# Cross-attention scores on TensorE: from six stacked bf16 parts on 96 rows to three fp32r parts on 48 rows, with two heads in the two row halves of the array

## The chip, the cores and the metric

One core of a Trainium2 chip runs the program. The metric is the device time of one execution in microseconds; lower is better. The engines are named as in the profile: PE (TensorE, with PEld for its weight loads), DVE (VectorE), ACT (ScalarE), POOL (GpSimd), SP (SyncE, which here only issues DMAs).

## The reference, cut to what matters

Four batches of 512 rows of 256 features go through an attention layer and then a mixture of experts with a shared expert. The attention keys and values come from a context (1601 rows, of which the causal mask leaves the first 512 in use).

```
Q = (layernorm(x) @ Wq.T + bq), K = (ctx @ Wk.T + bk), V = (ctx @ Wv.T + bv)   # 16 heads of 16
scores = einsum('bhqd,bhkd->bhqk', Q, K) / sqrt(16);  scores = where(causal, scores, -inf)
x = x + softmax(scores) @ V @ Wo.T + bo
logits = layernorm(x) @ gate_w.T;  two of eight experts per row, softmax weights
x = x + shared(layernorm(x)) + sum over the two experts of weight * (silu(g) * u) @ w_down[e].T
```

All tensors are fp32. The scores are wanted near fp32 precision, which is why Q and K are split into parts of lower precision whose products are added up.

## The kernel before

The program is written engine by engine, with semaphores set by hand; the order of the work on each engine is the order of the code. It has a prologue (loads, layer norm, transposes, first projections), the attention of the four batches (batches 0 to 2 in a hardware loop `Fori`, batch 3 as the final one), the router, and the expert stage.

**Groups and slots.** The 16 heads are four groups of four. A batch has four slots; in slot g PE makes the scores of group g, the row maxima of group g + 1, and P times V of group g - 1. The order inside is written out by hand in `SLOT` (L312): "R" is a row-maximum job, "S" a scores job, "PV" a quarter of P times V, "MAX" the maxima.

**The parts.** A projection of a half (128 features, two groups) lands in PSUM; DVE adds the bias (`values`, L1211) into `val`. ACT rounds it to bf16 (`part1`, L983), POOL subtracts (`remainders`, L502), ACT rounds the rest (`part2`, L993), POOL subtracts again (`part3`, L507), so Q and K are three bf16 parts each. In the prologue DVE makes the subtractions (L1218, L1223) between its row maxima. SP copies the parts by DMA from SBUF to SBUF into `qstack` and `kstack` (`stack`, L380): six products of parts, 16 features each, are stacked on 96 rows, so that one matmul over 96 rows gives the whole score. That is 12 DMAs for one group. A projection is made in slots g = 1 and g = 3 (a "split slot" in what follows); its stacks for the two groups go out there and in the slot behind. SP works in order: in `batch` (L403) stacks and `max_rows` alternate.

**Row maxima.** `rowmax_scores` (L601) makes the scores of a query tile k with queries on the partitions, `w = (k + 1) * 128` keys wide, and adds the mask to the diagonal block by a second matmul of two bf16 constants (L611). Its jobs fill half of set A of PSUM, two banks: k = 3 and k = 2 two heads a job, k = 1 and k = 0 four heads: six jobs. DVE reduces each (`rowmax`, L1252), and `max_parts` (L1264) splits the negated maxima into three bf16 parts in four steps. `maxima` (L614) transposes them by four matmuls on the identity into a bank of set B; ACT copies that (`max_rows`, L1009); SP writes it by DMA into rows 96 to 98 of `qstack` (L392), against rows of ones in `kstack` (filled at L483). S0 of the next slot waits for that DMA (`max_in`, L709).

**Scores and P V.** `scoresT` (L623) makes the scores with keys on the partitions, over 99 rows, so the maximum is already subtracted; ACT takes the exponential of each job into `pT` (`exps`, L1018). There are 11 S jobs: 4 of one head 512 wide, 4 of one head 384 wide, 2 of two heads 256 wide, 1 of four heads 128 wide. B jobs (S and MAX) rotate over three banks, and job n waits until job n - 3 is read (`b_free`). POOL zeroes the diagonal blocks (L524), and `probs_v` (L633) multiplies with V in fp32, each of the four heads on its own 32 columns of the array. ACT copies that out at the place MAX_AT = 9 of its own order (`p_v`, then `max_rows`).

**Output stage** of a batch: transposes of the output (L790), division by the sums on DVE (L1318, L1320), V of the next batch (L651), transposes back in `A_TILES` groups of three, three and two (L799), and the output projection (L815). In the final batch ACT also rounds the down weights (`down_hi`, L1013).

## Time and profile before

| what | us |
|---|---|
| median of 3 runs | 526.19 (525.32 to 528.68) |
| the profiled execution | 527.34 |
| its span, first to last instruction | 525.6 |
| PE matmul busy | 461.9 (88%) |
| DVE busy | 315.5 (60%) |
| ACT busy | 209.9 (40%) |
| POOL busy | 192.6 (37%) |
| mean granted PE clock, share of full speed | 0.962 |

The shown length of a matmul includes the time in which its last columns run through the array, so matmuls overlap; what one costs in a stream is the distance from its start to the next one's start. A weight load (PEld) is shown beside the matmuls. "x8" on a timeline row means eight instructions merged, from the first start to the last end. A time in brackets is how long the engine was idle before, and who released it. An fp32 matmul shows as two records.

### The profile page before, as it was taken

What the parts mean: (1) busy time and instruction counts of PE and PEld (TensorE: products, weight loads), DVE (VectorE), ACT (ScalarE), POOL (GpSimd) and SP (SyncE); (2) the same over time, 40 slices, a digit from 0 to 9 for tenths busy, and PEclk for the clock granted to TensorE, in tenths of its full rate; (3) what the DMA queues carried; (4) which work ended last, traced back from release to release, by engine and by line L of the source; (5) the groups of instructions that cost most, each with busy time, mean ns of one, the idle gap of its engine ahead of it and who ended that gap; (6) DMA issues with size and microseconds to landing.
All of it is one profiled execution on the core that took longest, in us unless ns stands there. A gap on an engine that the chain in (4) does not pass through costs nothing.

```text
span 525.6 us, 9951 instructions
## 1 busy us (share of the span) xinstructions
PE 461.9 (88%) x2998; PEld 314.7 (60%) x2999; DVE 315.5 (60%) x655; ACT 209.9 (40%) x421; POOL 192.6 (37%) x196
## 2 busy tenths in 40 slices
PE   3636989799898998988869999999999999999993
PEld 1315434365443744355326355669999999999942
DVE  6756666546656375756655489585545555555537
ACT  1213555542656255641785343333223232323210
POOL 8003543311334143510230100313766676766430
PEclk9956999989999999999998999999999999999997
DMA  8521331131112412130059760102444434444379
GB/s 255 211 73 44 97 105 68 60 129 60 66 65 71 141 39 83 50 127 24 3 188 343 295 228 1 42 10 42 67 74 63 76 64 70 70 72 69 42 178 332
DMA packets 45575, 53.84 MB, mean 102 GB/s; under 512 B 7761, under 2 KB 41873, under 8 KB 44913
## 3 DMA queue, kind: packets, MB, share of 16 engines
q1 hardware_dynamic: 35360, 40.63, 22.7%
q0 software_dynamic: 7488, 10.31, 12.2%
q10 hardware_dynamic: 2704, 2.62, 1.4%
q8 instruction: 13, 0.21, 0.2%
q14 instruction: 10, 0.07, 0.0%
HBM read 27.09 MB, written 13.67 MB: 78 GB/s over the span
## 4 chain that ended last, share of the span: by engine, by line
PE 63%; DVE 8%; ACT 8%; DMA 7%; issue 6%; SPq 4%; POOL 2%; DVEq 0%; ACTq 0%; POOLq 0%
PE set_a L902 5%; PE set_a L904 5%; PE set_a L903 5%; PE set_a L609 5%; PE set_a L834 5%; PE set_a L660 4%; ACT attention L1028 4%; PE set_b L639 4%; SPq L389 4%; PE set_b L629 4%; DMA attention<-attention 3%; PE set_b L844 3%; PE set_b L921 3%; PE set_a L815 3%; PE set_b L923 2%
## 5 line engine op out<-in xcount | busy, mean ns | idle before, releaser
L1262 DVE TENSOR_REDUCE attention<-set_a 128x2 f32<-128x1024 f32 (+2 forms) x96 | 96.2, 1042 | 37.2 <-PE set_a L611 35.7
L1028 ACT ACTIVATE attention<-set_b 128x512 f32<-128x512 f32 (+1 forms) x176 | 87.9, 566 | 62.7 <-PE set_b L629 62.3
L524 POOL TENSOR_SCALAR_AFFINE_SELECT attention<-attention 128x512 f32<-128x512 f32 x64 | 41.7, 663 | 113.6 <-ACT attention L1028 113.5
L629 PE MATMUL set_b<-attention 99*128 99x512 bf16 (+3 forms) x256 | 60.9, 313 | 20.2 <-ACT attention L1028 9.8
L609 PE MATMUL set_a<-attention 96*128 96x512 bf16 (+3 forms) x256 | 64.4, 317 | 16.2 <-DVE attention L1262 8.4
L575 POOL DMA_INDIRECT sum_rows<-moe,token_of x39 | 61.8, 1585 | 44.0 <-issue 29.9
L567 POOL DMA_INDIRECT e_x<-normed_rows,token_of x39 | 39.4, 1011 | 65.6 <-DVE token_of L1468 39.2
L1133 ACT ACTIVATE moe<-set_a 128x384 f32<-128x384 f32 x39 | 19.1, 490 | 105.3 <-PE set_a L904 97.3
L609 PEld LDWEIGHTS set_a<-attention 96*128 96x128 bf16 x256 | 26.1, 102 | 57.0 <-DVE attention L1262 21.7
L1493 DVE TENSOR_TENSOR moe<-set_a,moe 128x384 f32<-128x384 f32 x39 | 21.8, 558 | 62.7 <-issue 39.5
L902 PE MATMUL set_a<-wup_hi,e_xT_hi 128*128 x156 | 53.2, 341 | 0.0
L904 PE MATMUL set_a<-wup_hi,e_xT_lo 128*128 x156 | 52.8, 339 | 0.0
L903 PE MATMUL set_a<-wup_lo,e_xT_hi 128*128 x156 | 52.8, 338 | 0.0
L611 PE MATMUL set_a<-maskb,identb 128*128 128x128 bf16 x256 | 51.6, 229 | 0.0
L639 PE MATMUL set_b<-attention 128*32 128x128 f32 (+3 forms) x512 | 45.9, 460 | 0.7 <-ACT attention L974 0.7
L629 PEld LDWEIGHTS set_b<-attention 99*128 99x128 bf16 x256 | 19.7, 100 | 44.6 <-ACT attention L1028 24.2
L660 PE MATMUL set_a<-attention 128*128 (+1 forms) x64 | 30.8, 625 | 9.1 <-DMA attention<-in_ctxT 7.9
L921 PE MATMUL set_b<-w_down_hi,e_hT_hi 128*128 x117 | 36.5, 312 | 1.1 <-DVE moe L1505 0.9
L974 ACT ACTIVATE attention<-set_b 12x512 bf16<-12x512 f32 (+4 forms) x48 | 25.8, 598 | 26.9 <-PE set_b L803 13.2
L974 ACT ACTIVATE attention<-attention 128x512 bf16<-128x512 f32 x32 | 19.5, 645 | 39.8 <-DVE attention L1214 31.1
L923 PE MATMUL set_b<-w_down_hi,e_hT_lo 128*128 x117 | 32.9, 282 | 0.0
L922 PE MATMUL set_b<-w_down_lo,e_hT_hi 128*128 x117 | 32.9, 281 | 0.0
...
## 6 DMA issues: line engine op xcount, KB each, us to landing
...
```

Source lines behind the costliest of these rows:

```text
L575: g.indirect_dma_start(acc[i], bass.IndirectOffsetOnAxis(token_of[:, t:t + 1], 0), e_y[:, t % 2, :], None, compute_op=ALU.add).then_inc(ad ...
L609: mm(dst, qstack[0:ROWS, g // 2, h, k * P:w], kstack[0:ROWS, g // 2, h, 0:w], start=True, stop=False)
L611: last = mm(dst[:, k * P:w], identb[:], maskb[:], start=False, stop=True)
L629: last = mm(bank(par)[:, i * w:(i + 1) * w], kstack[0:ROWS + 3, g // 2, h, k * P:(k + 1) * P], qstack[0:ROWS + 3, g // 2, h, k * P:S], sta ...
L639: last = mm(pv_bank[32 * h:32 * h + 32, k * P:S], vaug[:, k, HG * g + h, :], pT[k][:, h, :], start=k == 0, stop=k == QT - 1, tile_position ...
L660: last = mm(pair(A, par)[:, a, :], w[:, c, half * P:(half + 1) * P], src[:, c, bass.ds(b * S, S)], start=c == 0, stop=c == C - 1)
L902: mm(dst, e_xT_hi[:, a, c, :], wup_hi[:, c, cols], start=c == 0, stop=False)
L903: mm(dst, e_xT_hi[:, a, c, :], wup_lo[:, c, cols], start=False, stop=False)
L904: last = mm(dst, e_xT_lo[:, a, c, :], wup_hi[:, c, cols], start=False, stop=c == C - 1)
L921: mm(dst, e_hT_hi[:, a, m, :], wdn_hi[:, m, cols], start=m == 0, stop=False)
L1028: nc.scalar.activation(pT[k][:, h:h + heads, :], bank(par)[:, 0:heads * (S - k * P)], ACT.Exp).then_inc(b_free, 1)
L1262: v.tensor_reduce(dst, src, AX.X, ALU.max, negate=True).then_inc(a_free, 1)
```

## The change

1. Q and K are split into two parts in fp32r, high and low: one ACT copy (`hi_parts_of`) and one subtraction (`low_parts`). The stack has three products (high-high, low-high, high-low) of 16 features: 48 rows. `part2`, `part3` and their waits are gone. The packing of the weights (`by_group`) changes so that a group's heads lie in pairs.
2. Two heads share the array: heads of the upper pair lie on rows 0 to 47 of `qstack` and `kstack`, those of the lower on rows 64 to 111. `rowmax_scores` issues the matmuls of two heads one behind the other, each on its row half and into its own PSUM bank, then their two mask matmuls over all rows. A stack is again 12 DMAs of a group, of 32 source rows of fp32.
3. The maxima are split into two fp32r parts; their rows are 48 and 49 of each half, over 50 rows in `scoresT`; two DMAs instead of one carry them.
4. There are 12 S jobs, each on one row half; the one of four heads at k = 3 becomes two of two. `SLOT` is reordered: S0, S1, S2 follow R2 without a row-maximum job between them.
5. `kstack` is filled whole with ones before the stacks; SP waits for that once (`fills`). `identr`, a copy of the identity in fp32r, is made by ACT in the prologue; PE waits for it once. `A_TILES` is two groups of four. `probs_v` takes its heads in the new order, and S0 waits for 2 x 16 more of `max_in` per slot. The stacks lie at fixed fp32r tensors in the same region.

The diff, cut to its core, blank lines left out and most lines moved left:

```diff
@@ -70,10 +70,11 @@
...
     SCALE = float(DK) ** -0.5
-    Q_PART = (0, 0, 1, 1, 0, 2)
-    K_PART = (0, 1, 0, 1, 2, 0)
+    Q_PART = (0, 1, 0)
+    K_PART = (0, 0, 1)
     ROWS = DK * len(Q_PART)
-    assert S == 512 and D == 256 and H == 2 * HH and ROWS == 96
+    HIGH = P // 2
+    assert S == 512 and D == 256 and H == 2 * HH and ROWS == 48 and HG == 4
@@ -163,17 +175,10 @@
...
 pT = [pT_all[:, pT_at[k]:pT_at[k + 1]].rearrange("p (h q) -> p h q", h=HG) for k in range(QT)]
-qstack = part(2 * HH * S // 2).bitcast(BF16).rearrange("p (a h n) -> p a h n", a=2, h=HH)
-kstack = part(2 * HH * S // 2).bitcast(BF16).rearrange("p (a h n) -> p a h n", a=2, h=HH)
+part(STACKS)
 val = part(2 * S).rearrange("p (a n) -> p a n", a=2)
-rem = part(2 * S).rearrange("p (a n) -> p a n", a=2)
-parts = part(2 * 3 * S // 2).bitcast(BF16).rearrange("p (a i n) -> p a i n", a=2, i=3)
-mneg = part(QT * HG).rearrange("p (k h) -> p k h", k=QT)
-mrem = part(QT * HG).rearrange("p (k h) -> p k h", k=QT)
-mparts = part(QT * 3 * HG // 2).bitcast(BF16).rearrange("p (k i h) -> p k i h", k=QT, i=3)
-mrows = part(S // 2).bitcast(BF16)
+mneg = part(QT * HG).rearrange("p (k a r) -> p k a r", k=QT, a=2)
 vaug = part(QT * H * 32).rearrange("p (k h w) -> p k h w", k=QT, h=H)
@@ -282,36 +287,23 @@
 stored = sem("stored")
-def heads_in_pair(k):
-    return max(2, min(HG, 1024 // ((k + 1) * P)) & ~1)
-def heads_in_bank(k):
-    return 1 if k < 2 else min(HG, 512 // (S - k * P))
-R_JOBS = [(k, h, heads_in_pair(k)) for k in range(QT - 1, -1, -1) for h in range(0, HG, heads_in_pair(k))]
+R_JOBS = [(3, (0,)), (3, (1,)), (2, (0,)), (2, (1,)), (1, (0, 1)), (0, (0, 1))]
 A_GRP = len(R_JOBS)
...
 A_ALL = A_PRO + B * A_PER - 2 * A_GRP - 3
-S_JOBS = [(k, h, heads_in_bank(k)) for k in range(QT) for h in range(0, HG, heads_in_bank(k))]
+S_JOBS = [(k, a, pr, 1 if k < 2 else 2) for k in range(QT)
+          for pr in (range(2) if k < 2 else range(1)) for a in range(2)]
 S_N = len(S_JOBS)
 B_SLOT = S_N + 1
-SLOT = [("R", 0), ("PV", 0), ("R", 1), ("PV", 1), ("R", 2),
-        ("S", 0), ("R", 3), ("S", 1), ("R", 4), ("S", 2), ("S", 3), ("R", 5), ("S", 4), ("S", 5),
-        ("S", 6), ("S", 7), ("PV", 2), ("PV", 3), ("S", 8), ("MAX", 0), ("S", 9), ("S", 10)]
+SLOT = [("R", 0), ("PV", 0), ("R", 1), ("PV", 1), ("R", 2), ("S", 0), ("S", 1), ("S", 2), ("R", 3),
+        ("S", 3), ("R", 4), ("S", 4), ("R", 5), ("S", 5), ("S", 6), ("S", 7), ("PV", 2), ("PV", 3),
+        ("S", 8), ("MAX", 0), ("S", 9), ("S", 10), ("S", 11)]
 LOGITS_IN = [A[:, 0, :], A[:, 1, :], pv_bank, A[:, 0, :]]
@@ -319,7 +311,7 @@
...
 assert [n for kind, n in SLOT if kind == "S"] == list(range(S_N))
-A_TILES = [range(i, min(i + 3, C * QT)) for i in range(0, C * QT, 3)]
+A_TILES = [range(i, i + 4) for i in range(0, C * QT, 4)]
 NA = len(A_TILES)
@@ -379,21 +371,24 @@
     def stack(g, u):
-        half, mine = g // 2, slice(g % 2 * 64, g % 2 * 64 + 64)
-        heads = slice(g % 2 * HG, g % 2 * HG + HG)
-        for part, made in enumerate((part1_ready, part2_ready, parts_ready)):
+        for part, (made, src) in enumerate(((hi_ready, qk_hi), (lo_ready, qk_lo))):
             for a, (dst, order) in enumerate(((qstack, Q_PART), (kstack, K_PART))):
...
                 for j, part_of in enumerate(order):
-                    if part_of == part:
-                        sp.dma_start(dst[DK * j:DK * (j + 1), half, heads, :],
-                                     parts[mine, a, part, :]).then_inc(rows_in[g], DMA)
+                    for high in range(2):
+                        if part_of == part:
+                            to, frm = HIGH * high + DK * j, HIGH * (g % 2) + 32 * high
+                            sp.dma_start(dst[to:to + DK, 2 * g:2 * g + 2, :].bitcast(F32),
+                                         src[frm:frm + 32, a, :].bitcast(F32)).then_inc(rows_in[g], DMA)
     def max_rows(g, n):
         sp.wait_ge(b_free, n + 1)
-        h = g % 2 * HG
-        sp.dma_start(qstack[ROWS:ROWS + 3, g // 2, h:h + HG, :], mrows[0:3 * HG, :]).then_inc(max_in, DMA)
+        for high in range(2):
+            to = HIGH * high + ROWS
+            sp.dma_start(qstack[to:to + 2, 2 * g:2 * g + 2, :].bitcast(F32),
+                         mrows[HG * high:HG * (high + 1), :].bitcast(F32)).then_inc(max_in, DMA)
+    sp.wait_ge(fills, 1)
     stack(0, 0)
@@ -480,7 +475,7 @@
     pool.wait_ge(consts, 4)
-    g.memset(kstack[ROWS:P], 1.0).then_inc(fills, 1)
+    g.memset(kstack[:].bitcast(F32), 1.0).then_inc(fills, 1)
     pool.wait_ge(fills, 1)
@@ -499,25 +494,16 @@
...
         pool.sem_inc(pool_turns)
-    def remainders(u):
+    def low_parts(u):
         for a in range(2):
-            pool_turn(part1_ready, 2 * u + a + 1)
-            g.tensor_tensor(rem[:, a, :], val[:, a, :], parts[:, a, 0, :], ALU.subtract).then_inc(rem_ready, 1)
-    def part3(u):
-        for a in range(2):
-            pool_turn(part2_ready, 2 * u + a + 1)
-            g.tensor_tensor(parts[:, a, 2, :], rem[:, a, :], parts[:, a, 1, :],
-                            ALU.subtract).then_inc(parts_ready, 1)
+            pool_turn(hi_ready, 2 * u + a + 1)
+            g.tensor_tensor(qk_lo[:, a, :], val[:, a, :], qk_hi[:, a, :], ALU.subtract).then_inc(lo_ready, 1)
     def mask_group(n, last=False, split=None):
         if split is not None:
-            remainders(split)
+            low_parts(split)
         for k in range(QT):
-            if k == 2 and split is not None:
-                part3(split)
             jobs = sum(job[0] <= k for job in S_JOBS)
@@ -600,15 +586,16 @@
     def rowmax_scores(g, j, n, par):
         pe.wait_ge(a_free, n - 1)
-        k, h0, heads = R_JOBS[j]
+        k, prs = R_JOBS[j]
         w = (k + 1) * P
-        in_bank = heads // 2 if k else HG
-        for i in range(heads):
-            h = g % 2 * HG + h0 + i
-            dst = pair(A, par)[:, i // in_bank, i % in_bank * w:(i % in_bank + 1) * w]
-            mm(dst, qstack[0:ROWS, g // 2, h, k * P:w], kstack[0:ROWS, g // 2, h, 0:w],
-               start=True, stop=False)
-            last = mm(dst[:, k * P:w], identb[:], maskb[:], start=False, stop=True)
+        for i, pr in enumerate(prs):
+            for high in range(2):
+                rows = slice(HIGH * high, HIGH * high + ROWS)
+                mm(pair(A, par)[:, high, i * w:(i + 1) * w], qstack[rows, 2 * g + pr, k * P:w],
+                   kstack[rows, 2 * g + pr, 0:w], start=True, stop=False, tile_position=(HIGH * high, 0))
+            for high in range(2):
+                last = mm(pair(A, par)[:, high, i * w + k * P:(i + 1) * w], identb[:], maskb[:],
+                          start=False, stop=True)
         last.then_inc(a_full, 1)
     def maxima(n, par, g_count, first=False):
@@ -616,18 +603,19 @@
...
         for k in range(QT):
-            last = mm(bank(par)[0:3 * HG, k * P:(k + 1) * P],
-                      mparts[:, k].rearrange("p i h -> p (i h)"), identb[:], start=True, stop=True)
+            last = mm(bank(par)[0:2 * HG, k * P:(k + 1) * P],
+                      mparts[:, k].rearrange("p a i r -> p (a i r)"), identr[:], start=True, stop=True)
         last.then_inc(b_full, 1)
     def scoresT(g, j, n, par):
         pe.wait_ge(b_free, n - 2)
-        k, h0, heads = S_JOBS[j]
+        k, high, pr, heads = S_JOBS[j]
         w = S - k * P
+        rows = slice(HIGH * high, HIGH * high + ROWS + 2)
         for i in range(heads):
-            h = g % 2 * HG + h0 + i
-            last = mm(bank(par)[:, i * w:(i + 1) * w], kstack[0:ROWS + 3, g // 2, h, k * P:(k + 1) * P],
-                      qstack[0:ROWS + 3, g // 2, h, k * P:S], start=True, stop=True)
+            last = mm(bank(par)[:, i * w:(i + 1) * w], kstack[rows, 2 * g + pr + i, k * P:(k + 1) * P],
+                      qstack[rows, 2 * g + pr + i, k * P:S], start=True, stop=True,
+                      tile_position=(HIGH * high, 0))
         last.then_inc(b_full, 1)
     def probs_v(g, count, k):
@@ -637,7 +625,7 @@
...
             last = mm(pv_bank[32 * h:32 * h + 32, k * P:S], vaug[:, k, HG * g + h, :],
-                      pT[k][:, h, :], start=k == 0, stop=k == QT - 1, tile_position=(0, 32 * h))
+                      pT[k][:, h % 2 * 2 + h // 2, :], start=k == 0, stop=k == QT - 1, tile_position=(0, 32 * h))
         if k == QT - 1:
@@ -988,37 +977,33 @@
...
             act.wait_ge(*((val_ready, u + 1), (a_free, n + 1))[a])
-            copy(parts[:, a, 0, :], val[:, a, :]).then_inc(part1_ready, 1)
-    def part2(u):
-        for a in range(2):
-            act.wait_ge(rem_ready, 2 * u + a + 1)
-            copy(parts[:, a, 1, :], rem[:, a, :]).then_inc(part2_ready, 1)
+            copy(qk_hi[:, a, :], val[:, a, :]).then_inc(hi_ready, 1)
     def ln_copy(b):
...
     ln_copy(0)
-    part1(0, 0)
-    part2(0)
+    hi_parts_of(0, 0)
+    act.wait_ge(consts, 1)
+    copy(identr[:], ident[:]).then_inc(identr_ready, 1)
     deviations(1, QT, T)
-    part1(1, 1, ((0, 1), 1))
-    part2(1)
+    hi_parts_of(1, 1, ((0, 1), 1))
     def max_rows(n, par):
         act.wait_ge(b_full, n + 1)
-        copy(mrows[0:3 * HG, :], bank(par)[0:3 * HG, :]).then_inc(b_free, 1)
+        copy(mrows[0:2 * HG, :], bank(par)[0:2 * HG, :]).then_inc(b_free, 1)
     def down_hi(i):
...
         copy(down_piece(wdn_hi, i), down_piece(wdn, i)).then_inc(dn_hi, 1)
-    def exps(n, par, pv=None, rows=True, split=None, down={}):
-        for j, (k, h, heads) in enumerate(S_JOBS):
+    def exps(n, par, pv=None, rows=True, down={}):
+        for j, (k, high, pr, heads) in enumerate(S_JOBS):
+            h = 2 * high + pr
             if pv and j == MAX_AT:
@@ -1215,24 +1197,18 @@
...
             last.then_inc(a_free if a else val_ready, 1)
-    def remainders(u):
+    def low_parts(u):
         for a in range(2):
-            dve.wait_ge(part1_ready, 2 * u + a + 1)
-            v.tensor_tensor(rem[:, a, :], val[:, a, :], parts[:, a, 0, :], ALU.subtract).then_inc(rem_ready, 1)
-    def part3(u):
-        for a in range(2):
-            dve.wait_ge(part2_ready, 2 * u + a + 1)
-            last = v.tensor_tensor(parts[:, a, 2, :], rem[:, a, :], parts[:, a, 1, :], ALU.subtract)
-            last.then_inc(parts_ready, 1)
+            dve.wait_ge(hi_ready, 2 * u + a + 1)
+            v.tensor_tensor(qk_lo[:, a, :], val[:, a, :], qk_hi[:, a, :], ALU.subtract).then_inc(lo_ready, 1)
     statistics(0)
...
     values(0, 0, 0)
-    remainders(0)
-    part3(0)
+    low_parts(0)
+    dve.wait_ge(lo_ready, 2)
     values(1, 1, 1)
     def add_v(n, par):
@@ -1250,37 +1226,26 @@
...
     def rowmax(j, n, par):
-        k, h, heads = R_JOBS[j]
+        k, prs = R_JOBS[j]
         dve.wait_ge(a_full, n + 1)
-        if k:
-            src = pair(A, par)[:, :, 0:heads // 2 * (k + 1) * P].rearrange("p a (h n) -> p a h n",
-                                                                         h=heads // 2)
-            dst = mneg[:, k, h:h + heads].rearrange("p (a h) -> p a h", a=2)
-        else:
-            src = pair(A, par)[:, 0, :].rearrange("p (h n) -> p h n", h=HG)
-            dst = mneg[:, k, :]
-        v.tensor_reduce(dst, src, AX.X, ALU.max, negate=True).then_inc(a_free, 1)
+        src = pair(A, par)[:, :, 0:len(prs) * (k + 1) * P].rearrange("p a (r n) -> p a r n", r=len(prs))
+        v.tensor_reduce(mneg[:, k, :, prs[0]:prs[0] + len(prs)], src, AX.X, ALU.max,
+                        negate=True).then_inc(a_free, 1)
     def max_parts(n, g_count):
         dve.wait_ge(a_free, n)
-        s0 = (g_count - 1) * 3
-        v.tensor_copy(mparts[:, :, 0, :], mneg).then_inc(mpart_step, 1)
-        dve.wait_ge(mpart_step, s0 + 1)
-        v.tensor_tensor(mrem, mneg, mparts[:, :, 0, :], ALU.subtract).then_inc(mpart_step, 1)
-        dve.wait_ge(mpart_step, s0 + 2)
-        v.tensor_copy(mparts[:, :, 1, :], mrem).then_inc(mpart_step, 1)
-        dve.wait_ge(mpart_step, s0 + 3)
-        v.tensor_tensor(mparts[:, :, 2, :], mrem, mparts[:, :, 1, :], ALU.subtract).then_inc(mparts_ready, 1)
+        hi = mparts[:, :, :, 0, :]
+        v.tensor_copy(hi, mneg).then_inc(mpart_step, 1)
+        dve.wait_ge(mpart_step, g_count)
+        v.tensor_tensor(mparts[:, :, :, 1, :], mneg, hi, ALU.subtract).then_inc(mparts_ready, 1)
     for g in range(2):
...
             if g == 0 and j == 1:
-                remainders(1)
-            if g == 0 and j == 3:
-                part3(1)
+                low_parts(1)
         max_parts(3 + (g + 1) * A_GRP, g + 1)
```

## Rows read from the trace of the kernel before

**Rows 1.** The page: busy by engine; the chain that ended last

```profile
PE 461.9 (88%) x2998; PEld 314.7 (60%) x2999; DVE 315.5 (60%) x655; ACT 209.9 (40%) x421; POOL 192.6 (37%) x196
PE 63%; DVE 8%; ACT 8%; DMA 7%; issue 6%; SPq 4%; POOL 2%; DVEq 0%; ACTq 0%; POOLq 0%
```

**Rows 2.** Windows: length, busy us (PE, PEld, DVE, ACT, POOL), clock, DMA share, GB/s

```profile
97.60:112.40 14.80, 12.17 (x88) 5.70 (x85) 6.98 (x10) 6.68 (x15) 3.77 (x6) 0.77 0.24 81
161.10:172.20 11.10, 9.53 (x89) 4.44 (x86) 6.93 (x10) 6.61 (x15) 3.74 (x6) 1.00 0.27 95
```

**Rows 3.** Timeline of PE, batch 1: start, length in us, what was run

```profile
126.19 0.38 PE L609 MATMUL set_a<-attention 96*128 96x512 bf16 x1
126.41 0.22 PE L611 MATMUL set_a<-maskb,identb 128*128 128x128 bf16 x1
126.47 0.38 PE L609 MATMUL set_a<-attention 96*128 96x512 bf16 x1
126.69 0.22 PE L611 MATMUL set_a<-maskb,identb 128*128 128x128 bf16 x1
126.84 1.07 PE L639 MATMUL set_b<-attention 128*32 128x512 f32 x8
135.00 0.39 PE L619 MATMUL set_b<-identb,attention 128*12 128x128 bf16 x4
136.51 0.38 PE L609 MATMUL set_a<-attention 96*128 96x512 bf16 x1
```

**Rows 4.** Waits: us in total, times, longest

```profile
PE set_b L629 <- DMA attention<-attention: 9.3, 7, 2.5
PEld set_b L629 <- ACT attention L1028: 24.2, 50, 1.2
```

**Rows 5.** Timeline of all engines, same slot and the next start

```profile
127.72 5.98 DVE L1262 TENSOR_REDUCE attention<-set_a 128x2 f32<-128x1024 f32 x6
134.54 1.19 ACT L974 ACTIVATE attention<-attention 128x512 bf16<-128x512 f32 x2
135.48 2.27 POOL L510 TENSOR_TENSOR attention<-attention 128x512 bf16<-128x512 f32 x2
139.11 0.79 SPq L395 DMA_DIRECT2D attention<-attention  x1
141.43 0.39 PE L629 MATMUL set_b<-attention 99*128 99x512 bf16 x1 [1.22 <-DMA attention<-attention]
```

**Rows 6.** Timeline of all engines, end of the slot from 136.51 on

```profile
146.32 0.39 PE L619 MATMUL set_b<-identb,attention 128*12 128x128 bf16 x4
146.92 1.05 ACT L974 ACTIVATE attention<-set_b 128x512 f32<-128x512 f32 x2
147.31 1.08 PE L660 MATMUL set_a<-attention 128*128 x2
147.99 0.75 SPq L395 DMA_DIRECT2D attention<-attention  x1
```

**Rows 7.** Timeline of PE: 8-row transposes, then a full-array matmul

```profile
300.78 0.41 PE L746 MATMUL set_a<-ident,moe 8*128 8x8 f32 x4 [0.68 <-ACT moe L974]
301.12 1.13 PE L834 MATMUL set_a<-moe,w_sg 128*128 128x512 f32 x2
```

**Rows 8.** Timeline of PE in the expert stage, fp32r matmuls of 256 columns

```profile
420.81 0.38 PE L921 MATMUL set_b<-w_down_hi,e_hT_hi 128*128 x1
421.02 0.28 PE L922 MATMUL set_b<-w_down_lo,e_hT_hi 128*128 x1
421.14 0.28 PE L923 MATMUL set_b<-w_down_hi,e_hT_lo 128*128 x1
```

**Rows 9.** Timeline of POOL and DVE in the prologue

```profile
3.11 6.92 POOL L483 MEMSET attention<- 32x8192 bf16 x1
...
39.94 1.28 DVE L1226 TENSOR_TENSOR attention<-attention 128x512 bf16<-128x512 f32 x2
```

**Rows 10.** Timeline of PE, start of a slot in the final batch

```profile
254.89 0.38 PE L609 MATMUL set_a<-attention 96*128 96x512 bf16 x1
```

33 lines of the change are left out of this document (21 added, 12 removed).

## The prediction

> **What bounds the kernel now.** I read the page first, then the windows by stage, then TensorE's timeline inside one attention slot, then the list of waits. The page gives TensorE 88% of the span and the chain that ended last puts 63% on it [rows 1]. The change touches attention alone, which ends near 276 us, so everything behind it stays. In attention one batch is four slots of 10.3 to 11.1 us (161.1 to 172.2 is one, 126.19 to 136.51 another [rows 2, 3]) and an output stage.
>
> Inside a slot TensorE goes in order through row-maximum jobs (R), scores jobs (S), probabilities times V (PV) and the maxima. Its prices, from starts in [rows 3]: a bf16 matmul of 512 columns takes 0.22 us (126.19 to 126.41), a mask matmul of 128 columns 0.06 (126.41 to 126.47). From the last mask (126.69, done streaming at 126.75) to PV (126.84) lie 0.09 us in which nothing streams: the array goes from all columns to four groups of 32. PV's eight records are two passes of four heads that start together, about 0.43 each at 512 columns: tiles of the array do run side by side here. So R0, PV0, R1, PV1, R2 up to S0 are 0.56 + 0.85 + 0.56 + 0.64 + 0.45, and four switches of 0.09: 3.4 us. From R0 to the end of the last maxima matmul (I call that M; a 128-column matmul is shown with 0.17 us behind its streaming, so M is 135.22) are 9.0 us.
>
> Two slots of each looped batch hold a wait on top. PE's wait for the DMA of the maxima rows is 9.3 us over 7 times; its loads wait for ACT's exps for 24.2 us, 1.5 a slot over 16 slots [rows 4]. Its cause is in [rows 5]: ACT makes the second parts at 134.54, GpSimd the third at 135.48 (2.27 us), only then can SyncE issue the last stack DMAs, and the maxima row DMA queued behind them goes at 139.11; S0 starts at 141.43 after a 1.22 us wait. In batch 0 the wait was the longest (2.5 us), and the granted clock of that stretch is 0.77 against 1.00 [rows 2]: 14.8 us where the same slot of batch 1 took 11.1. That slot lost 3.7 us more, about 1.3 of it wait and 2.4 the 1.2 GHz level that the clock fell to after the idle time.
>
> **Removed from the path.** No second pair of copies on ACT (1.3 us of a split slot's 2.6), no third part on GpSimd, two of four DVE steps of the maxima. The stack DMAs stay 12 per unit and 64 KB each, so SyncE still issues 12 x 0.64 us, but the last four wait for GpSimd's single subtraction, which can end about 3 us after ACT's first copies start; the third parts end at 137.75, more than 7 us later. The maxima DMA (two now, +0.64 us of issue) then starts when ACT's copy is done. In [rows 6] that copy pair (0.45 + 0.6) ends at 147.97, 1.4 us after M (146.54); two issues and a 2.2 us landing give S0 at M + 4.4, while PE needs until about M + 5.2. So the waits go: 1.2 us in each of six slots, and in batch 0 the 3.7.
>
> **Added on TensorE.** A pair of fp32r matmuls on the two row halves, then two full-array masks. Does a change of row grouping cost a gap like the column one? The only case is in [rows 7]: transposes on 8 rows, the last starting at 300.78 + 0.41 - 0.20 = 300.99 with 8 columns to stream, then a full-array matmul that waits for nothing, at 301.12: 0.13 us, of which the 8 columns explain at most some 0.03. I take 0.09 per switch; bounds 0 and 0.13. fp32r costs 0.12 us per 256 columns [rows 8], so 0.24, 0.18, 0.12, 0.06 for 512 to 128; and where the weight load could not go ahead (420.81) the next matmul came after 0.21, not 0.12: 0.09 to 0.10 us for an exposed load, bounds 0 and 0.10. Masks with their bf16 load: 0.13 a pair.
>
> By this, two heads cost 0.24/0.18/0.12/0.06 + 0.09 + 0.13, and 0.09 + 0.10 to come back to the row mode: 0.65, 0.59, 0.53, 0.47 us, against 0.56, 0.45, 0.34, 0.23 now. Over eight pairs of a slot: 4.5 against 3.2, less two PV switches that were paid already (0.2): +1.1 us. Loads exposed at S8 and S9: +0.2. Scores stream 5,120 columns at 0.47 against 0.43 ns, less one pair that overlaps (S0, S1; the others are apart in the order or gated by ACT): no change. Work +1.3 us a slot.
>
> The Trainium skill, TensorEngine Tiling (Array Packing), Key Properties, states that changing the tiling mode, not just the tile, drains TensorE. The 0.09 us of [rows 3, 7] agree with it; by a reading without drains the sum would be the first rival's. The same skill, TensorE: Matmul & The Clock Gate, Weight-path perf modes, keeps the fast weight load from fp32 operands; the 0.10 us of [rows 8] agrees.
>
> Last, an added wait. There are 12 S jobs rather than 11, over three banks, so S11 reuses the bank of the maxima and must wait for ACT's copy, M + 1.4 by [rows 6]. Behind it in PE's queue are the projection and the next R0. Now they start at M + 0.8 (147.31); then at M + 1.6: +0.8. In split slots (g = 1, 3) the second copies already delay ACT; the next R0 comes at M + 1.3 (136.51), so +0.3.
>
> **Sum.** R0 to S0 is then 3.55 us. From S0 to M: S0 to S2 0.48, R3 and back 0.59, S3 0.24, R4 1.06, S4 0.18, R5 0.94, S5 to S7 0.54, PV2 and PV3 with both switches 0.88 and a load 0.10, S8, switch and maxima 0.57: 5.6. R0 to M is 9.15 of work, against 9.0 of which some 0.9 was waiting for ACT, which the new work takes up; an unsplit slot (136.51 to 146.54, less its 1.22 wait) took 8.8. So a split slot is +0.15 + 0.3, +0.45. Slot g = 2: +0.35 + 0.8 - 1.2, 0. Slot g = 0, where the output stage starts after ACT's PV copy, 1.1 behind M now and 1.6 then: +0.35 + 0.5 - 1.15, -0.3. Output stage, two transposed groups instead of three: -0.1. A batch: +0.5. Batches 1 and 2: +1.0; batch 0: +0.5 - 3.7 = -3.2. Prologue: the two part-3 subtractions (1.28) and half of the small steps go [rows 9], but the R4 and R5 behind run at 1.2 GHz with the added switches: -0.5. Its larger-looking fill of kstack is 4,096 four-byte elements a partition where 8,192 took 6.92 us from 3.11, long before the first stack at 19 us: 0. Final batch, no split, ACT also makes w_down_hi: R0 started at 254.89 right after S10 [rows 10]; S11 waits for the copy that ends near 255.5, so +0.85 for two slots and +0.2 in the third: +1.9. Total +1.0 - 3.2 - 0.5 + 1.9 = -0.8 us. The profiled execution took 527.34 us, 1.7 of it outside its span of 525.6, so by it the sum gives 526.5; it was 1.15 above the median of the runs, 526.19, so against that I forecast 525.4.
>
> **Rivals.** (A) No drain for row groups and loads prefetched: 14 added switches x 0.09 and 10 loads x 0.10, 2.3 us of PE work less a slot. DVE's six row maxima (6.0 us [rows 5]) and S11 then bound it: unsplit slots gain 1.6, six times, the others 0.5, nine times: 525.4 - 14 = 511. For: no row shows 64-row tiles. Against: [rows 7]. (B) The halves do not overlap: R streams 1.2 us more and S0/S1 0.24, in 16 slots: +22, 547. Against: PV's four tiles start together. (C) Slower through the clock: array streaming in a slot falls from about 7.7 us to 6.3 of 10.7, more gaps; if the granted clock falls as it did at 103 us, at 2.4 us each, in two slots of each of the three looped batches, +14: 539. It decides once the clock is below 1.00 in slots where nothing waits. For: the dip of [rows 2]. Against: waits of 1.2 us made none. (D) The ACT and GpSimd chain, not PE, sets the split slots: 1.3 us of copy, 0.4 of DVE and the waits of S6, S7 and S10 go, the new work fits in: -1.3 in six slots: 517.5. For: PE's loads wait 1.5 us a slot for ACT. Against: the work is at 8.1 us of 9.0 there before 1.1 is added ahead of M.
>
> **Numbers.** Forecast 0.45, A 0.15, B 0.10, C 0.15, D 0.15. The forecast's own range is 519 to 532. Low 512 takes in D and half of A, high 543 takes in C and leaves B out. A measurement tells about 1% here, 5.3 us. Faster: A, D and a little of the forecast, 0.33; slower: B, C and a little, 0.29; within 1%: 0.38.
>
> **What would show it.** Granted clock 1.00 through 97 to 112 us and that slot near 11; no PE wait for the maxima DMA; last R matmul to first mask 0.09 us more than streaming; a pair's two starts within some 0.01 us; PE waiting for ACT's copy ahead of the last S job; split slots near 10.8, slot g = 2 near 10.8. If masks follow without a gap, A holds; if the second head starts a stream later, B; if the clock row is below 1.00 in looped batches, C. Slots under 10 us or over 12 make the prediction wrong.

## The result and the profile after

| | median us | runs | ratio to the kernel before, 95% interval |
|---|---|---|---|
| before | 526.68 | 525.32 to 528.68 | |
| after | 563.51 | 555.61 to 567.16 | 1.0646 [1.053, 1.0763] |

The change makes the kernel 6.5% slower; the forecast was 525.4 and its range ended at 543. The four executions of the kernel after took 567.16, 563.90, 563.12 and 555.61 us at a mean granted clock of 0.876, 0.884, 0.885 and 0.905: the lower the clock, the longer the time. The profiled one is the slowest of them, 3.6 us above the median, and its losses are read with that in mind. The granted clock is the share of full speed that TensorE was given, between 1.00 (2.4 GHz) and 0.50 (1.2 GHz); a value between them is the mean of a stretch that had both.

The page of the kernel after: busy times, the row of the granted clock (40 slices of the span, in tenths), the chain that ended last, and the groups of the row maxima, their masks and the scores.

```profile
PE 518.2 (92%) x2998; PEld 347.0 (61%) x2999; DVE 304.9 (54%) x619; ACT 204.5 (36%) x418; POOL 177.5 (31%) x184
...
PEclk9957699559658899986958799999999999999998
...
PE 78%; ACT 6%; DMA 4%; DVE 4%; issue 3%; SPq 3%; DVEq 0%; ACTq 0%; POOLq 0%
...
L594 PE MATMUL set_a<-kstack,qstack 48*128 48x512 f32 (+3 forms) x256 | 70.8, 448 | 15.0 <-DVE attention L1232 7.8
L616 PE MATMUL set_b<-qstack,kstack 50*128 50x256 f32 (+3 forms) x256 | 76.8, 456 | 8.2 <-ACT mrows L963 5.6
```

PE has as many instructions as before (2998), is 56 us longer busy, and its share of the chain went from 63% to 78% [rows 1]. No other engine took anything over: DVE, ACT and POOL are all less busy. So it is PE that runs longer, and the clock row says how. In the kernel before it reads

```profile
PEclk9956999989999999999998999999999999999997
```

with one dip inside attention. After, 14 of the first 23 slices are below 9. Two stretches of the same length in both, batch 0 and batch 1 (columns: start and end, length, busy us of PE, PEld, DVE, ACT and POOL, granted clock, DMA share, GB/s). The kernel before:

```profile
66.00:118.00 52.00, 45.91 (x353) 23.80 (x352) 28.89 (x45) 28.30 (x58) 17.61 (x23) 0.93 0.26 89
118.00:172.00 54.00, 49.54 (x377) 24.39 (x375) 33.76 (x50) 29.13 (x61) 17.75 (x22) 1.00 0.19 66
```

The kernel after, with three shorter stretches:

```profile
66.00:118.00 52.00, 50.55 (x319) 23.77 (x317) 28.21 (x34) 24.39 (x51) 13.20 (x17) 0.83 0.28 70
118.00:172.00 54.00, 53.17 (x267) 30.83 (x265) 20.94 (x31) 19.34 (x41) 9.53 (x13) 0.66 0.21 59
...
98.90:145.00 46.10, 45.52 (x238) 26.74 (x239) 20.52 (x30) 15.94 (x34) 7.61 (x10) 0.70 0.25 71
...
101.00:112.00 11.00, 10.74 (x59) 4.58 (x60) 3.28 (x6) 3.83 (x9) 1.91 (x3) 0.50 0.26 63
...
239.00:250.00 11.00, 10.44 (x87) 5.34 (x86) 7.76 (x10) 6.96 (x14) 3.78 (x4) 1.00 0.30 72
```

The last two are the same kind of work, 11 us each: at clock 1.00 PE gets 87 matmuls done in them, at 0.50 (the 1.2 GHz level) 59. And in the slow one PE is not idle: it is busy for 10.74 of 11.00 us. This is the main reading of the case: the clock is at its lower level although PE works without a pause.

Where the 39.8 us of span went (565.4 less 525.6). Slots are counted here from R0 to the next R0, where in the kernels with row halves R0 starts with the second matmul of its pair; slot g = 2 thus includes the projection of the slot behind it. 4.8 us were lost before the first row maxima of slot g = 1 of batch 0 (50 to 62.7 us is at clock 0.62, where it was at 1.00 before), 29.1 in the twelve slots from there to the final batch's slot g = 1, 2.5 in that slot and 3.4 behind it. Where a slot ran at clock 1.00 throughout it is near the forecast: a split slot 11.00 us against 10.31 before, slot g = 2 with the projection 14.66 against 14.28. Where it did not, the same slots took up to 12.92 (clock 0.76) and 22.79 (0.54). At the end of a split slot the first matmul of the pair starts 0.18 us ahead of the second, beside the last scores job on the other row half (249.80 and 249.98 below). Counted to that first start the two slots are 10.82 and 14.85 us; their sum is the same to 0.01 us.

Inside a slot at full clock. The timeline of PE in the kernel after, slot g = 3 of batch 2:

```profile
238.97 0.50 PE L594 MATMUL set_a<-kstack,qstack 48*128 48x512 f32 x2
239.41 0.28 PE L597 MATMUL set_a<-maskb,identb 128*128 128x128 bf16 x2
239.62 1.06 PE L627 MATMUL set_b<-attention 128*32 128x512 f32 x8
240.62 0.51 PE L594 MATMUL set_a<-kstack,qstack 48*128 48x512 f32 x2
...
242.64 0.73 PE L616 MATMUL set_b<-qstack,kstack 50*128 50x512 f32 x3
...
248.01 0.41 PE L606 MATMUL set_b<-identr,mparts 128*8 128x128 f32 x4
248.34 0.86 PE L616 MATMUL set_b<-qstack,kstack 50*128 50x256 f32 x4
249.71 0.32 PE L616 MATMUL set_b<-qstack,kstack 50*128 50x128 f32 x1 [0.51 <-ACT mrows L963]
249.80 0.49 PE L594 MATMUL set_a<-kstack,qstack 48*128 48x512 f32 x1
...
249.98 0.44 PE L594 MATMUL set_a<-kstack,qstack 48*128 48x512 f32 x1
```

Two heads together take 0.50 us; shown one by one at the start of the next slot they take 0.49 and 0.44: the row halves do run side by side. From the pair's start to the first mask are 0.44 us, of which streaming is 0.24. S0 comes 3.67 us behind R0, the maxima are done at 248.01 + 0.41 - 0.17 = 248.25, and PE then stands idle for 0.51 us before the last scores job. The list of waits of the kernel after agrees (us in total, times, longest):

```profile
PE set_b L616 <- ACT mrows L963: 5.6, 14, 0.5
PE set_b L616 <- ACT attention L1013: 1.9, 5, 0.6
```

There is no wait for the DMA of the maxima rows in it, which was 9.3 us before [rows 4]; the new wait for ACT's copy is 5.6 us over 14 slots.

### The profile page after: what moved, and what is told of

Read it like the earlier page. It is cut to its first block, busy times and chain, and to the rows that moved or that the text cites. A ratio compares the mean times of both kernels' runs of the same rounds, so it can differ in the third digit from the quotient of the medians.

```text
span 565.4 us, 9891 instructions
## 1 busy us (share of the span) xinstructions
PE 518.2 (92%) x2998; PEld 347.0 (61%) x2999; DVE 304.9 (54%) x619; ACT 204.5 (36%) x418; POOL 177.5 (31%) x184
## 3 DMA queue, kind: packets, MB, share of 16 engines
q0 software_dynamic: 7488, 10.31, 11.5%
## 4 chain that ended last, share of the span: by engine, by line
PE 78%; ACT 6%; DMA 4%; DVE 4%; issue 3%; SPq 3%; DVEq 0%; ACTq 0%; POOLq 0%
PE set_b L627 9%; PE set_b L616 9%; PE set_a L594 7%; PE set_a L648 6%; PE set_a L597 5%; PE set_a L891 5%; PE set_a L893 5%; PE set_a L892 5%; PE set_a L823 4%; PE set_b L833 3%; PE set_b L910 3%; PE set_a L804 3%; SPq L381 2%; PE set_b L912 2%; ACT attention L1013 2%
## 5 line engine op out<-in xcount | busy, mean ns | idle before, releaser
L1232 DVE TENSOR_REDUCE attention<-set_a 128x2 f32<-128x1024 f32 (+2 forms) x96 | 98.4, 1044 | 62.1 <-PE set_a L597 61.0
L594 PE MATMUL set_a<-kstack,qstack 48*128 48x512 f32 (+3 forms) x256 | 70.8, 448 | 15.0 <-DVE attention L1232 7.8
L616 PE MATMUL set_b<-qstack,kstack 50*128 50x256 f32 (+3 forms) x256 | 76.8, 456 | 8.2 <-ACT mrows L963 5.6
L594 PEld LDWEIGHTS set_a<-kstack,qstack 48*128 48x128 f32 x256 | 34.8, 217 | 54.8 <-DVE attention L1232 27.8
L616 PEld LDWEIGHTS set_b<-qstack,kstack 50*128 50x128 f32 x256 | 41.7, 233 | 30.6 <-ACT attention L1013 10.2
L627 PE MATMUL set_b<-attention 128*32 128x128 f32 (+3 forms) x512 | 58.2, 566 | 0.0
L648 PE MATMUL set_a<-attention 128*128 (+1 forms) x64 | 36.4, 721 | 8.4 <-DMA attention<-in_ctxT 7.3
L597 PE MATMUL set_a<-maskb,identb 128*128 128x128 bf16 x256 | 41.2, 250 | 0.0
L597 PEld LDWEIGHTS set_a<-maskb,identb 128*128 128x128 bf16 x256 | 15.3, 102 | 29.8 <-issue 25.4
L1196 DVE TENSOR_SCALAR attention<-set_a,attention 128x512 f32<-128x512 f32 x16 | 11.3, 747 | 38.9 <-PE set_a L648 38.8
```

The lines of the kernel that those rows point to most:

```text
L594: mm(pair(A, par)[:, high, i * w:(i + 1) * w], qstack[rows, 2 * g + pr, k * P:w], kstack[rows, 2 * g + pr, 0:w], start=True, stop=False, t ...
L597: last = mm(pair(A, par)[:, high, i * w + k * P:(i + 1) * w], identb[:], maskb[:], start=False, stop=True)
L616: last = mm(bank(par)[:, i * w:(i + 1) * w], kstack[rows, 2 * g + pr + i, k * P:(k + 1) * P], qstack[rows, 2 * g + pr + i, k * P:S], start ...
L627: last = mm(pv_bank[32 * h:32 * h + 32, k * P:S], vaug[:, k, HG * g + h, :], pT[k][:, h % 2 * 2 + h // 2, :], start=k == 0, stop=k == QT - ...
L648: last = mm(pair(A, par)[:, a, :], w[:, c, half * P:(half + 1) * P], src[:, c, bass.ds(b * S, S)], start=c == 0, stop=c == C - 1)
L1232: v.tensor_reduce(mneg[:, k, :, prs[0]:prs[0] + len(prs)], src, AX.X, ALU.max, negate=True).then_inc(a_free, 1)
```

## Experiments: what lowers the clock

The theory that I began with (C1): the clock falls because of the short gaps that 14 changes of array mode and 10 exposed weight loads put into each slot. Its rivals: the number of array rows that work (C2: 48 and 50 of 128 in the new matmuls, 96 and 99 before), the wait of the last scores job, and fp32r itself. Where a kernel below runs the matmuls of a pair over the rows of both halves, it leaves out the right scores: both heads get the sum of the two. Such a kernel is there to be timed only.

**Both matmuls over the rows of both halves.** The query stack is filled with zeros and the unused rows 48 to 63 of the key stack too.

```diff
-                        rows = slice(HIGH * high, HIGH * high + ROWS)
+                        rows = slice(0, HIGH + ROWS)
                         mm(pair(A, par)[:, high, i * w:(i + 1) * w], qstack[rows, 2 * g + pr, k * P:w],
-                           kstack[rows, 2 * g + pr, 0:w], start=True, stop=False, tile_position=(HIGH * high, 0))
+                           kstack[rows, 2 * g + pr, 0:w], start=True, stop=False)
...
-                rows = slice(HIGH * high, HIGH * high + ROWS + 2)
+                rows = slice(0, HIGH + ROWS + 2)
```

> After, but every score matmul runs over all rows of both halves (rows 0 to 111 and 0 to 113), without a tile position: same columns, same weight loads, no change of row mode, no overlap of two heads. Both heads of a pair get the sum of their scores. Theory C (the clock): the halves lower the activity of the array, so here the granted clock goes back to 0.95 or more and the time to 515 to 528 us. Rival 'the added wait of the last scores job lets the clock fall': that wait is still in, clock stays below 0.91, time over 545.

Measured: 533.0 us (531.72 to 538.62), ratio 1.0142 [1.0065, 1.0218]. The windows of this kernel:

```profile
66.00:118.00 52.00, 48.69 (x369) 30.55 (x368) 30.62 (x40) 27.86 (x60) 15.05 (x20) 1.00 0.35 85
118.00:172.00 54.00, 52.00 (x359) 32.99 (x358) 31.31 (x39) 25.25 (x53) 13.17 (x17) 1.00 0.29 79
```

The clock is back at 1.00 in both, and 30 of the 37 us are back, though 533.0 is 5 us over the range expected for theory C. fp32r and the stacks of three products stay in this kernel, so they are not the cause. It does not yet part gaps from rows: the mode changes went along with the half rows.

**No mask matmuls**, which takes the changes of mode out and leaves the halves.

```diff
-                        mm(pair(A, par)[:, high, i * w:(i + 1) * w], qstack[rows, 2 * g + pr, k * P:w],
-                           kstack[rows, 2 * g + pr, 0:w], start=True, stop=False, tile_position=(HIGH * high, 0))
-                    for high in range(2):
-                        last = mm(pair(A, par)[:, high, i * w + k * P:(i + 1) * w], identb[:], maskb[:],
-                                  start=False, stop=True)
+                        last = mm(pair(A, par)[:, high, i * w:(i + 1) * w], qstack[rows, 2 * g + pr, k * P:w],
+                                  kstack[rows, 2 * g + pr, 0:w], start=True, stop=True, tile_position=(HIGH * high, 0))
```

> After without the 256 mask matmuls of the row maxima (the maxima are then taken over keys that are masked later as well; the softmax comes out the same). It takes out 12 of the switches of row mode per slot and 0.9 us of masks, and leaves two heads in the halves. Theory C1 (the clock falls through the gaps at the switches): clock 0.95 or more, time 505 to 515. Theory C2 (it falls because only half of the rows work in a scores matmul and two row-maximum matmuls overlap, so less of the array streams): masks were full-array work, so the clock stays at or below 0.90 and the time is 535 to 550.

Measured: 552.28 us (552.00 to 553.06), 1.0486 [1.0441, 1.0531]. The windows of this kernel:

```profile
66.00:118.00 52.00, 49.83 (x266) 24.40 (x266) 25.88 (x34) 25.62 (x57) 13.53 (x18) 0.63 0.27 67
118.00:172.00 54.00, 52.42 (x273) 30.24 (x273) 27.46 (x38) 21.64 (x46) 12.48 (x16) 0.75 0.26 70
```

A split slot at clock 1.00 took 9.56 us, 1.44 less than in the kernel after and 0.75 less than before: that is what the masks and the switches to them cost on the path. But the mean clock is 0.839 to 0.842 in all four executions, lower than the 0.876 to 0.905 with the gaps in. C1 falls: most of the gaps went and the clock went down, as C2 has it, since the masks are the matmuls that use all 128 rows. The time is 2 us above the range expected for C2, on the side of more loss.

**The maxima one scores job later**, so that the last job does not wait for ACT.

```diff
-                ("S", 8), ("MAX", 0), ("S", 9), ("S", 10), ("S", 11)]
+                ("S", 8), ("S", 9), ("MAX", 0), ("S", 10), ("S", 11)]
...
-        MAX_AT = 9
+        MAX_AT = 10
```

> After with the maxima one job later (behind S9), so that the last scores job no longer waits for ACT's copy. The wait of 0.8 us a slot goes. If the wait is what lets the clock fall: clock 0.95, time 515. If not (C1, C2): clock 0.88 to 0.90, time lower by 16 x 0.8 = 13 us at most, 550 to 560.

Measured: 558.01 us (551.05 to 563.26), 1.0513 [1.0429, 1.0597], mean clock 0.866 in its profile and 0.874 to 0.906 in the other three executions. The split slot at clock 1.00 fell from 11.00 to 10.53 us, so the wait was worth 0.5 us there, where the forecast had counted 0.3 for a split slot and 0.8 for g = 2. The clock did not come back; the wait is not its cause.

**Scores over both halves, row maxima in halves**, the second edit of the first experiment alone, with its zeros.

```diff
-                rows = slice(HIGH * high, HIGH * high + ROWS + 2)
+                rows = slice(0, HIGH + ROWS + 2)
...
-                              qstack[rows, 2 * g + pr + i, k * P:S], start=True, stop=True,
-                              tile_position=(HIGH * high, 0))
+                              qstack[rows, 2 * g + pr + i, k * P:S], start=True, stop=True)
```

> After, with only the scores matmuls (S) over the rows of both halves (both heads of a pair get the sum of their scores there); the row-maximum matmuls stay in the halves, with as many switches per slot as after. C2: S is 40% of what streams and goes from half the rows to all, clock 0.93 or more, time under 545. C1: number of gaps unchanged, clock as after, 0.87 to 0.91, time 553 to 567.

**Row maxima over both halves, scores in halves**, the first edit alone (there the key stack keeps its ones).

```diff
-                        rows = slice(HIGH * high, HIGH * high + ROWS)
+                        rows = slice(0, HIGH + ROWS)
```

> After with the row-maximum matmuls over the rows of both halves, one after the other (their maxima are of other sums of scores), and the scores matmuls left in their halves of 50 rows. Counterpart of e4. If a matmul on half of the rows is what lowers the clock, wherever it stands: clock 0.93 or less, and not above e4's 0.954. If it is the overlap of two row-maximum matmuls: clock 0.95 or more here. Time 535 to 545 with the clock up, 550 or more with it down.

Measured: 545.39 us (543.89 to 547.59), 1.0353 [1.0299, 1.0407] with the scores full; 560.81 us (557.67 to 566.92), 1.0604 [1.0545, 1.0664] with the row maxima full. The windows, scores full:

```profile
66.00:118.00 52.00, 50.00 (x319) 25.16 (x318) 26.28 (x34) 26.12 (x58) 14.41 (x19) 0.92 0.30 76
118.00:172.00 54.00, 51.62 (x344) 30.02 (x342) 30.16 (x41) 23.89 (x52) 13.13 (x17) 1.00 0.28 76
...
98.90:145.10 46.20, 44.49 (x288) 25.00 (x286) 26.84 (x35) 18.87 (x39) 10.65 (x13) 0.96 0.29 80
```

and row maxima full:

```profile
66.00:118.00 52.00, 50.48 (x294) 24.71 (x294) 24.80 (x30) 21.73 (x46) 12.80 (x17) 0.86 0.27 66
118.00:172.00 54.00, 52.09 (x312) 30.66 (x312) 26.21 (x37) 22.29 (x48) 10.09 (x15) 0.94 0.25 67
```

With the row maxima still in halves, all their mode changes are still there, and the clock is 0.92 and 1.00, its mean 0.950 to 0.960. The scores jobs use one half each, so but for S0 and S1 they stream on 50 rows with the other half idle, and they cost the most clock. But they are not alone. With only the row maxima full the mean clock is 0.912 to 0.935, where the kernel after has 0.876 to 0.905. The time hardly gains from it, because the two matmuls of a pair no longer run side by side: a split slot at clock 1.00 is about 1.1 us longer. And in the stretch around the start of attention the clock comes back only when both are full. Scores full, then both full:

```profile
50.00:72.00 22.00, 20.07 (x81) 13.25 (x80) 8.14 (x13) 10.71 (x18) 11.42 (x5) 0.61 0.34 82
...
50.00:72.00 22.00, 19.68 (x114) 12.52 (x113) 12.37 (x18) 12.23 (x21) 13.80 (x7) 0.96 0.39 96
```

In the profiles of this case every kernel with either kind of matmul in halves has 0.59 to 0.69 in that stretch; those with neither have 0.77 to 1.00. So row maxima in pairs on the two halves cost clock too, though less.

**Every mask twice**: more work and no fewer gaps.

```diff
-                    for high in range(2):
-                        last = mm(pair(A, par)[:, high, i * w + k * P:(i + 1) * w], identb[:], maskb[:],
-                                  start=False, stop=True)
+                    for again in range(2):
+                        for high in range(2):
+                            last = mm(pair(A, par)[:, high, i * w + k * P:(i + 1) * w], identb[:], maskb[:],
+                                      start=False, stop=again == 1)
```

> After with every mask matmul issued twice: 16 more full-array matmuls of 128 columns a slot, 0.9 us each slot at full clock, 14 us in all; no more switches. If the clock follows how much of the array streams (C2): clock up from 0.88 to 0.92 or more, and the time stays within 8 us of after's 563. If it does not: 575 us or more at a clock of 0.88.

Measured: 557.74 us (557.17 to 569.36), 1.0566 [1.0541, 1.0591], mean clock 0.931 or 0.932 in four executions and 0.909 in the fifth, which is the profiled one and the longest. A slot at clock 1.00 is 0.8 us longer (11.78 against 11.00 us), some 13 us over 16 slots, and the time is no longer than that of the kernel after. Windows of its batch 1 and of the final batch:

```profile
118.00:172.00 54.00, 52.10 (x381) 30.62 (x381) 29.27 (x39) 23.69 (x51) 12.51 (x16) 1.00 0.28 75
...
247.00:300.00 53.00, 50.82 (x301) 30.75 (x293) 23.16 (x30) 19.40 (x38) 5.73 (x9) 0.69 0.11 31
```

The added matmuls on all rows bring the clock back in most of the looped batches (0.92 for the first stretch of the other kernels, 66 to 118 us). Over the final batch it is 0.69 in this profile. That says little: the other four executions are 11 to 12 us shorter at a higher clock, and no trace shows where.

**Rows or tiles?** The last rival to C2: not the number of rows but the confinement to a half of the array. This kernel has the same instructions as the one with full scores, and its scores matmuls are full-array ones too, but over 66 rows. It leaves out all but two rows of the upper half, so its scores are not the right ones either.

```diff
-                rows = slice(0, HIGH + ROWS + 2)
+                rows = slice(0, HIGH + 2)
```

> As the kernel in which the score products read the rows of both halves and the row maxima stay in row halves (545.4 us, mean clock 0.954, every slot of the three looped batches but one at 1.00), with one thing changed: the score products are full-array matmuls over rows 0 to 65, not 0 to 113, so 66 rows carry data instead of 114, and no matmul changes its mode for it (they compute the lower half's scores plus 16 rows of zeros: the sums of heads are left out). Theory C-rows (the clock falls with the number of rows that carry data): the clock falls again in the slots, mean 0.90 to 0.93, time 550 to 560. Theory C-tile (the clock falls with matmuls that are confined to a half of the array, each of which leaves the other half idle): the clock stays at 0.95 or over and the time at 543 to 548. The warm slots cost the same by both (11.4 for a split slot).

Measured: 571.96 us (569.66 to 578.31), 1.0844 [1.08, 1.0887]. Windows of this kernel:

```profile
66.00:118.00 52.00, 50.41 (x296) 24.04 (x296) 24.70 (x30) 22.24 (x48) 13.86 (x18) 0.83 0.26 66
118.00:172.00 54.00, 52.41 (x299) 31.76 (x298) 24.54 (x34) 21.66 (x46) 10.07 (x14) 0.83 0.25 67
...
98.90:145.10 46.20, 45.68 (x234) 27.69 (x232) 20.38 (x29) 15.41 (x32) 7.62 (x10) 0.70 0.25 70
```

48 rows fewer under the same instructions: the clock falls from 0.92 and 1.00 to 0.83 and 0.83, over 98.9 to 145.1 us from 0.96 to 0.70, and the time rises by some 26 us, more than either theory had said. The two were run at different times; the kernel before took 526.9 us beside the one and 525.73 beside the other. Fewer rows in full-array matmuls are enough to lower the clock, with no half tile in them and no added gap: C2 is shown. What is not shown is that tiles add nothing: the mean clock with 66 rows (0.876 to 0.895) is about that of the kernel after (0.876 to 0.905), where the scores have 50.

## Experiments: a version that beats both

**The kernel before without masks.** The masks only keep the subtracted maximum to the keys that a query sees.

```diff
-                    mm(dst, qstack[0:ROWS, g // 2, h, k * P:w], kstack[0:ROWS, g // 2, h, 0:w],
-                       start=True, stop=False)
-                    last = mm(dst[:, k * P:w], identb[:], maskb[:], start=False, stop=True)
+                    last = mm(dst, qstack[0:ROWS, g // 2, h, k * P:w], kstack[0:ROWS, g // 2, h, 0:w],
+                              start=True, stop=True)
```

> The kernel before, without the 256 mask matmuls (maxima over keys that are masked later too; the softmax comes out the same). 16 matmuls of 0.057 us less a slot, 0.9 us. TensorE bound and clock kept: 512 to 518. If the clock falls with the work that goes, as in e2: 520 or more at a clock under 0.95.

Measured: 525.83 us (521.13 to 529.93), 0.9944 [0.9909, 0.9979], which is neither of the two outcomes expected: 8 us above the first, and at a clock that is under 0.95 in only five of the ten executions. A split slot went from 10.31 to 10.08, less than the masks' 16 x 0.06 us [rows 3], since PE then waits for DVE's row maxima more often (13 times, 11.0 us, where it was 7 times, 8.4 us). In the profile the dip of [rows 2] is gone, but the stretch from 50 to 72 us is at clock 0.77, where it was at 1.00.

**All rows, maxima later** (the first and third experiments together).

> e1 (full rows, sums of two heads) with the maxima one job later. The clock was at full in e1, so here the price of the added wait shows alone: 0.8 us in each of some 14 slots, 11 us: 522 us against e1's 533, clock 0.96. If the wait only moves to the next slot's first scores (the maxima row lands later), 528 to 533.

Measured: 529.58 us (526.72 to 534.63), 1.0063 [1.0025, 1.0101]. The expectation had 522 for a wait of 0.8 us a slot; the slots of batch 1 are 0.46 us shorter than in the first experiment (split 11.33 to 10.87, g = 2 14.07 to 13.61), so that was the wait's size. Even with its clock back and the new wait gone, this kernel is no faster than the one before: a split slot takes 10.87 us against 10.31. It does not have the overlap of the two heads, so it does not say what the layout with it would take at full clock.

**The row of maxima from ACT's own queue.** This tests the reading of [rows 5], on the kernel before: the DMA waits its turn behind stacks that are needed later.

```diff
             def max_rows(g, n):
-                sp.wait_ge(b_free, n + 1)
-                h = g % 2 * HG
-                sp.dma_start(qstack[ROWS:ROWS + 3, g // 2, h:h + HG, :], mrows[0:3 * HG, :]).then_inc(max_in, DMA)
+                pass
...
                 copy(mrows[0:3 * HG, :], bank(par)[0:3 * HG, :]).then_inc(b_free, 1)
+                act.wait_ge(b_free, n + 1)
+                h = g % 2 * HG
+                nc.scalar.dma_start(qstack[ROWS:ROWS + 3, g // 2, h:h + HG, :], mrows[0:3 * HG, :]
+                                    ).then_inc(max_in, DMA)
```

> The kernel before, with one edit: the DMA that puts the three rows of maxima into the query stack is issued by ScalarE right behind its own copy of them, not by SyncE, whose queue holds the stack rows of a later group ahead of it. Theory SP-order (the 1.2 us waits at the score products that end last on this DMA, 9.3 us over 7 of them in the profile of before, come from its place in SyncE's queue): those waits shrink to the transfer itself and the time falls by 3 to 7 us, to 519 to 524. Theory transfer (it is the transfer that takes long, and issuing it costs ScalarE 0.1 us a slot in front of its first exponentials): the waits stay, and the time is 525 to 529.

The same without the masks:

> The same edit on the kernel before without its mask matmuls (those are left out: the row maxima are taken over all keys of the diagonal tiles, and the softmax is the same for any value subtracted). The kernel before without masks took 525.83 in its run, 0.9944 of before. Theory SP-order: 3 to 7 us below that, 519 to 523, the waits at the score products on the DMA gone. Theory transfer: 525 to 528.

And on top of both, one bf16 part of the maximum (the copies, the DMA and the scores rows shrink with it):

```diff
...
-                v.tensor_copy(mparts[:, :, 0, :], mneg).then_inc(mpart_step, 1)
-                dve.wait_ge(mpart_step, s0 + 1)
-                v.tensor_tensor(mrem, mneg, mparts[:, :, 0, :], ALU.subtract).then_inc(mpart_step, 1)
...
-                v.tensor_tensor(mparts[:, :, 2, :], mrem, mparts[:, :, 1, :], ALU.subtract).then_inc(mparts_ready, 1)
+                v.tensor_copy(mparts[:, :, 0, :], mneg).then_inc(mparts_ready, 1)
```

> The kernel of the run before, with the maximum rounded to one bf16 value and one row of it in the stack in place of three (the softmax divides by the sum of its own exponentials, so it is the same for a rounded maximum); three VectorE operations and their waits on one another go out of the chain between the last row maximum and the transposes, 8 rows are moved instead of 24. By the chain of waits (0.3 to 0.45 us for the three, in front of transposes that PE waits for in the slots where nothing else is left to issue): 2 to 5 us less than the run before if the transposes' wait is exposed in most of the 12 slots, 516 to 520; the same time within 1 us if the score products wait for the exponentials' buffers or the DMA anyway.

Measured: 520.11 us (518.74 to 520.89), 0.9886 [0.9858, 0.9915]; without masks 515.51 us (514.54 to 518.12), 0.9810 [0.9781, 0.9839]; with one part 514.44 us (511.47 to 515.08), 0.9769 [0.974, 0.9798]. In the first of the three, a timeline of ACT and PE in batch 1, the slot that starts at 133.09:

```profile
132.65 1.05 ACT L972 ACTIVATE attention<-set_b 128x512 f32<-128x512 f32 x2
133.72 0.75 ACTq L1012 DMA_DIRECT2D attention<-attention  x1
...
133.09 0.38 PE L607 MATMUL set_a<-attention 96*128 96x512 bf16 x1
...
136.63 0.38 PE L627 MATMUL set_b<-attention 99*128 99x512 bf16 x1
```

and its waits:

```profile
PE set_b L627 <- ACT attention L1030: 10.2, 29, 1.0
...
PE set_b L627 <- DMA attention<-attention: 0.9, 1, 0.9
```

The DMA goes 0.63 us behind R0, where it went 2.60 behind it before (139.11 less 136.51 [rows 3, 5]), S0 starts without a wait, 9.3 us of waits in seven places [rows 4] have become 0.9 in one, and slot g = 2 takes 13.24 us, not 14.29. The queue's order was the cause. Without the masks 515.51 us lies below the 519 to 523 expected. That range was counted down from 525.83 us of another time; by the ratios to the kernel before, each beside its own runs, the queue gives 7 us there (0.9944 to 0.9810), the upper end of the 3 to 7 us expected. The last step, one part for three, left every slot of the looped batches at its length within 0.01 us; its interval overlaps that of the kernel before it, so it is no gain that was shown. The last version is 2.3% faster than the kernel before, and 8.7% faster than the kernel after by the two medians.

## Why the prediction was wrong

**Right.** The waits for the maxima row are gone. The halves overlap (rival B is refuted: 0.50 us for two heads). A change of row mode and an exposed load cost what was taken: pair to mask is 0.44 us, against 0.24 + 0.09 + 0.10. R0 to S0 is 3.67 us (forecast 3.55), S0 to the maxima 5.6 (5.6), from there to the first start of the next R0 1.55 (1.6), with S11 waiting for ACT's copy as described. Rival A is refuted by the same rows, and D too, since split slots grew. The 0.10 us of an exposed load did not by itself show that fp32r weights load slower; the loads do: in the kernel before 128 columns took 102 ns in bf16 (L609) and 188 ns in fp32r (L902).

**Mis-sized.** A split slot at clock 1.00 is +0.69 and not +0.45; slot g = 2 is +0.38 and not 0. Over six and three slots that is 2.6 us. (Counted to the first start of R0 they are +0.51 and +0.57, and 2.1 us.) With these terms the sum is at most 525.4 + 2.6 = 528.0, within 1% of before.

**The step that failed** is that the sum prices the slots at full clock, and leaves the clock to rival C at too small a price and chance. The prediction gave the clock's fall a chance of 0.15, and 2.4 us in two slots of each looped batch, 14 us in all. The argument against it was "waits of 1.2 us made none", and the argument for it was the dip of [rows 2], which followed an idle time. Both look at idle time only. The paragraph did count that the streaming of the array falls "from about 7.7 us to 6.3 of 10.7", but read it as time with nothing in the array, never as how much of the array a streaming matmul uses. In its place the runs showed a clock that falls while PE is busy for 10.74 of 11.00 us, and that follows the rows: 0.92 and 1.00 in two windows with 114 rows under the scores, 0.83 in both with 66, under the same instructions. Rival C had the direction, but gaps as the cause: with the gaps of the masks taken out the mean clock fell to 0.842. A fall was seen in seven of the twelve slots of the looped batches, down to a mean of 0.54, and ahead of them. So the sum lost the -3.2 us of batch 0 as well, whose fourth slot was to gain its clock back: it was at 0.66 where before it had 0.88, and took 33.27 us, not 28.55.

The mean clock prices the loss, as an estimate from the runs: from 563.90 to 555.61 us the kernel's own executions differ by 0.021 of mean clock (0.884 to 0.905), 8.3 us. From the 0.885 of a median run to the 0.962 of before would be some 30 of the 37 us. The rest, some 7 us, is what the new layout costs at the clock of before. The forecast's -0.8 holds 2.4 us of clock given back in batch 0; without them it is +1.6, and with the mis-sized terms about +4. The first experiment ends 6 us above before as well, but its matmuls do not overlap and need no change of mode, so that is no confirmation.

The Trainium skill, TensorE: Matmul & The Clock Gate, What's actually happening, says that an activity monitor sets the share of clock pulses by how busy the array has been recently. If busy is read as the busy share of PE in the profile, the trace disagrees: 98% busy and half the pulses. Only if activity is read as work in the array does it agree with these runs; the page does not say which.

**Open.** A kernel in which all scores jobs come as pairs on the two halves was not run. It would test whether two half-array matmuls at once count like one on the whole array. What there is points both ways: with full scores and the row maxima in pairs the clock was 1.00 over 118 to 172 us, but 0.61 over 50 to 72 us, where it was 0.96 with both full. Nor was it tested how much a half tile costs beyond its fewer rows.
